# Inverse roots of two attentions: from powers on GpSimd to exponentials of half logarithms on ScalarE, products of ones in the early gaps, and new orders on four engines

## The reference

```python
x = x + layernorm(attention_A(layernorm(x)))
x = x + layernorm(stack_B(layernorm(x)))
```

```python
q = l2norm(q) * qs;  k = l2norm(k) * ksc        # t / max(norm(t), 1e-12)
q, k = rotary_xpos(q, k)
h = a * gelu(g, approximate=False)              # feed-forward part
```

## Time and profile before

| | us |
|---|---|
| median of 3 runs | 487.34 |
| lowest and highest | 486.87, 491.44 |
| the profiled execution | 492.14 |
| its span, first to last instruction | 490.3 |
| mean granted clock of TensorE, share of full speed | 0.979 |

### The profile page before, as it was taken

How to read it: one execution, slowest core, us unless ns; L and a number is a source line. 1 busy time by engine, 2 the same in 40 slices (tenths; PEclk the granted TensorE clock), 3 DMA queues, 4 the chain that set the end, 5 groups by cost and what they waited for, 6 DMA issues and landing times.

```text
span 490.3 us, 15662 instructions
## 1 busy us (share of the span) xinstructions
PE 452.1 (92%) x6258; PEld 288.7 (59%) x6258; DVE 380.0 (77%) x743; ACT 343.9 (70%) x901; POOL 320.7 (65%) x270
## 2 busy tenths in 40 slices
PE   7879989999989898999899999999998999998994
PEld 5656656656656565756455665565655655655662
DVE  3746675896898659989978788789688697877776
ACT  2136756575667898887768887887887788876832
POOL 4422150678559987999987986884978449773112
PEclk8879999999899999999999999999999999999998
DMA  6102022000001010010000000110000000101102
GB/s 192 45 3 47 14 86 47 5 10 17 3 4 24 3 24 1 4 23 1 23 3 23 23 3 21 23 23 3 23 1 23 1 23 1 23 2 24 23 1 86
DMA packets 13476, 11.42 MB, mean 23 GB/s; under 512 B 4210, under 2 KB 10716, under 8 KB 13404
## 3 DMA queue, kind: packets, MB, share of 16 engines
q1 hardware_dynamic: 13404, 10.42, 8.2%
HBM read 5.05 MB, written 1.05 MB: 12 GB/s over the span
## 4 chain that ended last, share of the span: by engine, by line
PE 57%; DVE 19%; ACT 9%; issue 8%; POOL 5%; DMA 2%; POOLq 0%; SPq 0%; DVEq 0%; ACTq 0%
PE bank L512 8%; PE bank L609 8%; PE bank L729 8%; ACT bank L1324 5%; PE bank L685 4%; PE bank L695 4%; DVE mx_a L1808 4%; PE bank L648 4%; PE bank L618 3%; PE bank L546 3%; PE bank L666 3%; PE bank L744 3%; DVE p_b L1890 2%; PE bank L629 2%; DVE rc L1864 2%
## 5 line engine op out<-in xcount | busy, mean ns | idle before, releaser
L2440 POOL TENSOR_TENSOR r_qk<-ss,minus_half 128x16 f32<-128x16 f32 x32 | 93.7, 2929 | 2.7
L1324 ACT ACTIVATE bank<-bank,mn_b 128x128 f32<-128x128 f32 x256 | 88.9, 363 | 3.1 <-DVE mn_b L1878 3.0
L2433 POOL TENSOR_TENSOR rc<-rc,rs 128x1024 f32<-128x1024 f32 x32 | 75.5, 2359 | 23.3 <-DVE rs L1870 23.3
L1808 DVE TENSOR_REDUCE mx_a<-bank 128x2 f32<-128x512 f32 (+1 forms) x96 | 61.3, 685 | 31.6 <-PE bank L523 31.1
L1277 ACT ACTIVATE pT_k<-bank 128x512 f32<-128x512 f32 x96 | 52.9, 598 | 34.8 <-PE bank L523 34.7
L2447 POOL TENSOR_TENSOR rc<-rc,r_qk 128x1024 f32<-128x1024 f32 x32 | 60.8, 1903 | 2.3
L609 PE MATMUL bank<-wqkv,xS 128*128 128x512 f32 x128 | 61.8, 605 | 0.3 <-DVE mx_a L1808 0.3
L1324 ACT ACTIVATION_READ_ACCUMULATOR bank<-bank,mn_b 128x1 f32 x256 | 58.8, 230 | 0.0
L512 PE MATMUL bank<-qT_a 32*128 32x256 f32 (+1 forms) x768 | 52.8, 368 | 4.2 <-ACT qT_a L1261 1.6
L1864 DVE TENSOR_TENSOR rc<-bank,tab_c 128x1024 f32<-128x1024 f32 x32 | 39.0, 1219 | 14.4 <-ACT sq L1299 14.0
L729 PE MATMUL bank<-yfT,w 128*128 128x512 f32 (+3 forms) x108 | 48.1, 559 | 0.4 <-ACT pT_b L1333 0.2
(11 more groups left out here) (136 smaller groups left out, 870.4 us busy)
## 6 DMA issues: line engine op xcount, KB each, us to landing
v_b<-v_b SPq DMA_DIRECT2D x32, 128.0 KB, 2.5
wqkv<-in_L_ffn_wqkv_dram SPq DMA_DIRECT2D x2, 768.0 KB, 5.6
x_all<-in_L_attn_x_dram SPq DMA_DIRECT2D x1, 768.0 KB, 5.6
out_dram<-pT_k SPq DMA_DIRECT2D x3, 256.0 KB, 2.3
w<-in_L_ffn_w_dram SPq DMA_DIRECT2D x2, 341.0 KB
wo<-in_L_ffn_wo_dram SPq DMA_DIRECT2D x2, 256.0 KB, 5.6
const<-consts_dram SPq DMA_DIRECT2D x1, 352.0 KB, 6.3
x_all<-in_L_attn_x_dram SPq DMA_DIRECT2D x1, 256.0 KB, 3.0
```

The costliest lines, as they stand in the source:

```text
L1324: m = s.activation(x, x, ACT.Exp, bias=mn_b[:, qt, c, p:p + 1], scale=-1.0, accum_out=sum_b[:, qt, c, p:p + 1])
L1808: v.tensor_reduce(mx_a[:, qt, h0:h0 + nh], full(src).rearrange("p (h k) -> p h k", h=nh), AX.X, ALU.max).then_inc(S("a_mx"), 1)
L2433: g.tensor_tensor(rc[:, k % 2, :, :], rc[:, k % 2, :, :], rs[:, k % 2, :, :], ALU.add).then_inc(S("b_add"), 1)
L2440: g.tensor_tensor(r_qk[:, n, :], ss[:, n, :], minus_half[:, :], ALU.pow).then_inc(S("b_r"), 1)
```

## The change

1. **Second attention's inverse norms.** DVE's b_norms takes the maximum with TINY itself, behind its sum. b_pow moves from POOL's list to ACT's: a logarithm in place, then an exponential with the scale -0.5.
2. **The two layer norms between the blocks.** a_z and a_h0 on POOL lose their powers; ACT has a_z_rs and a_h0_rs, each a logarithm and an exponential on 128x2.
3. **One table.** exps() loads the table that has both logarithm and exponential. It stands ten times in ACT's list, wherever such an operation follows other tables.
4. **Products of ones.** busy takes waits. Six calls of it are new in TensorE's list, with 2, 4, 3, 5, 2 and 2 products of 128 columns, all among the first three batches of the first attention.
5. **Orders.** The lists of TensorE, ScalarE, VectorE and GpSimd are new, and so are the banks. SP's list is the same. The powers of f_rs, last_rs and a_rs stay on POOL.

```diff
-            def busy(dst, n, cols):
+            def busy(dst, n, cols, *free):
+                for f in free:
+                    after(t, *f)
                 for _ in range(n):
                     t.matmul(full(dst)[:, 0:cols], ones[:, 0:PARTS], ones[:, 0:cols], start=True, stop=True)
...
+            def exps():
+                s.preload_act_table_set("natural_log_exp_and_others")
+            def a_z_rs(b):
+                s.wait_ge(S("a_ve0"), b + 1)
+                s.activation(rs2[0][:, :], ve2[0][:, :], ACT.Ln).then_inc(S("a_ln0"), 1)
+                s.wait_ge(S("a_ln0"), b + 1)
+                s.activation(rs2[0][:, :], rs2[0][:, :], ACT.Exp, scale=-0.5).then_inc(S("a_rs0"), 1)
...
+            def b_pow(k):
+                n = k % 2
+                s.wait_ge(S("b_ss"), k + 1)
+                s.activation(ss[:, n, :], ss[:, n, :], ACT.Ln).then_inc(S("b_ln"), 1)
+                s.wait_ge(S("b_ln"), k + 1)
+                after(s, *unit("b_qkr", k - 2))
+                s.activation(r_qk[:, n, :], ss[:, n, :], ACT.Exp, scale=-0.5).then_inc(S("b_r"), 1)
...
                 v.tensor_reduce(ss[:, n, :], sq[:, n, :].rearrange("p (h d) -> p h d", d=HD), AX.X, ALU.add)\
-                    .then_inc(S("b_ss"), 1)
+                    .then_inc(S("b_sum"), 1)
+                v.wait_ge(S("b_sum"), k + 1)
+                v.tensor_scalar(ss[:, n, :], ss[:, n, :], TINY, None, ALU.max).then_inc(S("b_ss"), 1)
...
             def a_z(b):
-                g.wait_ge(S("a_ve0"), b + 1)
-                g.tensor_tensor(rs2[0][:, :], ve2[0][:, :], minus_half[:, 0:TILES], ALU.pow).then_inc(S("a_rs0"), 1)
                 g.wait_ge(S("a_rs0"), b + 1)
...
-            def b_pow(k):
-                n = k % 2
-                g.wait_ge(S("b_ss"), k + 1)
-                g.tensor_scalar(ss[:, n, :], ss[:, n, :], TINY, None, ALU.max).then_inc(S("b_n2"), 1)
-                g.wait_ge(S("b_n2"), k + 1)
-                g.tensor_tensor(r_qk[:, n, :], ss[:, n, :], minus_half[:, :], ALU.pow).then_inc(S("b_r"), 1)
```

The new list of TensorE around the second batch of the first attention, and pieces of ACT's and DVE's:

```diff
+            a_turn_k(1, 7, of("a_mx", 0, 6, 12))
+            busy(0, 2, 128, of("a_mx", 0, 8, 12))
+            a_proj(2, 0)
+            busy(6, 4, 128, of("a_xnT_out", 2))
+            a_turn_m(0, 6)
+            busy(6, 3, 128, of("a_mT_out", 0), of("a_kT_out", 1))
+            a_turn_q(1, 3)
+            busy(7, 5, 128, of("a_qT_out", 1), of("a_rope", 2), of("a_mx", 0, 9, 12))
+            a_quad(1, 0, (7, 0, 5, 2))
...
+            b_proj(0, 0, of("a_exp", 2, 11, 12), of("a_mx", 3, 11, 12))
...
+            a_quad(4, 0, (7, 5, 3, 2), of("a_ov", 2, 0, 2), of("a_rope", 5), of("a_kT_out", 4))
...
             a_qT(1, 3)
+            exps()
+            a_exp(0, 0, 5)
...
+            f_gate(1, 1, 3)
+            exps()
+            b_pow(15)
+            b_pow(16)
...
+            b_rot(25, 3)
+            b_norms(25)
...
+            b_rot(26, 1)
+            b_norms(26)
```

More of the change, by code:

```diff
@@ L793, in _ @@
[L793 to L801, removed]
@@ L845, in _ @@
[L845 to L854, removed]
@@ new lines, in _ @@
+            a_values(4, 0, 7, of("a_rope", 7))
+            a_quad(5, 5, (6, 5, 0, 1), of("a_mx", 5, 7, 12), of("a_exp", 4, 8, 12), of("a_o", 3))
+            a_turn_q(6, 1, of("a_mx", 5, 9, 12))
+            a_values(4, 1, 7)
+            a_turn_o(3, 0, of("a_exp", 4, 10, 12))
+            a_turn_m(5, 6, of("a_mx", 5, 10, 12))
+            b_turn_qk(0, 1, of("a_qT_out", 6))
+            b_proj(2, 2, of("a_mx", 5, 11, 12))
+            b_v(2, 6, of("a_mT_out", 5))
+            a_values(4, 2, 3, unit("b_trT_out", 0))
@@ new lines, in _ @@
+            a_values(5, 1, 0)
+            a_h0(2, 6, of("a_exp", 5, 11, 12))
+            a_values(5, 2, 5, of("a_mx", 6, 9, 12))
+            a_turn_m(6, 1, of("a_mx", 6, 11, 12))
+            a_values(5, 3, 5)
+            b_v(3, 1, of("a_mT_out", 6))
+            a_turn_o(4, 4)
+            b_turn_p(0, 3, of("a_h0T_out", 2))
+            a_quad(7, 0, (4, 0, 5, 3), of("a_oT_out", 4), of("a_ov", 5, 1, 2), unit("b_p", 0))
+            b_turn_qk(2, 3, unit("b_pT_out", 0))
+            a_out(4, 1, unit("b_v", 3))
@@ new lines, in _ @@
+            b_turn_qk(5, 1, unit("b_o", 1), of("a_exp", 7, 4, 12))
+            a_turn_back(6, 0, of("a_exp", 7, 6, 12))
+            b_out(0, 7, of("a_yin", 5))
+            a_h0(4, 1, of("a_o", 6))
+            b_proj(6, 1, unit("b_trT_out", 5))
+            b_scores(3, 3, of("a_exp", 7, 7, 12), batch("b_x", 0))
+            b_turn_p(2, 0, of("a_h0T_out", 4))
+            b_proj(7, 0, unit("b_pT_out", 2))
+            b_values(2, 2)
+            b_v(5, 2, unit("b_rot", 6))
+            a_quad(8, 2, (3, 4, 7, 5), unit("b_o", 2), unit("b_p", 3))
@@ L1464, in _ @@
[L1464 to L1477 removed]
+            a_exp(1, 8, 1)
+            a_exp(1, 9, 2)
+            a_exp(1, 10, 4)
+            a_z_rs(0)
+            a_ov(1, 0, 3)
@@ new lines, in _ @@
+            a_exp(4, 5, 7)
+            a_h0T(1, 1)
+            a_kT(6, 5)
+            a_exp(4, 6, 3)
+            a_exp(4, 7, 2)
+            a_z_rs(2)
+            a_exp(4, 8, 5)
+            a_exp(4, 9, 4)
+            b_pow(1)
+            a_exp(4, 10, 0)
+            a_qT(6, 1)
+            a_exp(4, 11, 1)
+            a_ov(4, 0, 7)
+            a_oT(3, 0)
+            a_mT_out(5, 6)
+            b_qkT(0, 1)
+            b_sq(2, 2)
+            b_v(2, 6)
+            a_ov(4, 1, 3)
+            a_exp(5, 0, 6)
```

2201 lines of the change are left out of this document (1096 added, 1105 removed).

## The result

The changed kernel takes 500.8 us in the median of four runs (495.79 to 503.95), the kernel before beside it 488.1 us: a ratio of 1.0222 with a 95% interval of 1.0156 to 1.0288. The forecast was 481.7 us with a range up to 497: the time moved the other way, and it lies above the range. The first line is the engines' busy time, the second the chain of waits by engine.

A forecast was written before the change was run, and what follows sets the result against it. TensorE was taken as the bound, busy 452.1 of 490.3 us. Clock -2.1, 100 to 128 us -3.5, middle about 0 and tail 0 summed to -5.6 from the median of 487.34: 481.7 us, range 470 to 497.

The forecast's parts named there:

- item 3: Middle, 140 to 470 us: GpSimd's relief -5.7, VectorE's load +4.2, ScalarE's +3.0; net about 0, bounds -8 and +11.
- VectorE +22 x 0.19 = +4.2: Middle, 140 to 470 us: 22 us of maxima added on VectorE, weighted by its 19% share of the chain.
- rival C: VectorE's maximum waits for GpSimd's 128x1024 operations; half of 22 us reaches TensorE, 11 us more: 492.8 us; chance 0.20.
- item 1: Clock, 29 to 36 us: 2.7 us back from full-level quads, less the products' cost; net -2.1, bounds +1.3 and -3.3.
- Rival C's mark for VectorE's load: At 1.4 us per maximum for all units, VectorE has 314 us of work from 140 to 470, as much as TensorE.
- The seven units with the sum directly behind the rotation: Second attention's units 6, 9, 10, 20, 25, 26, 29: maximum waits for GpSimd's addition, 1.4 us each, 9.8 us.
- the six with one instruction between: Second attention's units 7, 8, 11, 13, 18, 19: maximum on VectorE at about 0.4 us each, 2.4 us.
- the other nineteen: Remaining units of the second attention: maximum put at L1834's mean, 0.53 us each, 10.1 us.
- Item 2: Stretch 100 to 128 us: TensorE's idle time and low clock, where two GpSimd powers stand; -3.5 us, bounds 0 and -4.
- The term for ScalarE (+3.0): Middle, 140 to 470 us: 33 us added on ScalarE by activation pairs and table loads, weighted by 0.09.
- Item 4: Tail: last gates, products, statistics and powers of last_rs stay; 0, within 2 us either way.
- Rival D: ScalarE at 90% in strict order makes late items delay all behind; 9.6 us more arrive: 491.3 us; chance 0.08.

The follow-up runs named there:

- No maximum at all: Changed kernel without VectorE's maximum with TINY, the reduction itself releasing ScalarE's logarithm: 484.0 us, ratio 0.9897 to the kernel before.

## Why the prediction was wrong, point by point

**The step that failed** is in item 3 of the sum: "VectorE +22 x 0.19 = +4.2". The mechanism was foreseen, the maximum waiting for GpSimd's 128x1024 operations, and so were its 22 us on VectorE (21.4); what was wrong is the weight. 15.5 of 21.4 us arrived, 0.72 each. With +15.5 in place of +4.2 the sum is +5.7, rival C's outcome; measured is +11.2 against the runs of before beside it (499.6 - 488.4). Of the rest, 2.1 us are item 1, of which nothing was there; more than that is not placed. Two things were wrong in the weight.

First, 0.19 is VectorE's share in the chain over the whole kernel. An average share says how often the end passed through that engine, not what a microsecond added in one place will cost. From 200 to 240 us VectorE had 3.2 us left, and with the maxima there 0.85. Rival C's mark for VectorE's load, 314 us of work in 330, was read over the long stretch and so was never reached on paper. The weight depends on the place: by the estimate under "No maximum at all" all of the waits between units 2 and 12 arrive, and about half of those behind unit 12; in the old order with the power on GpSimd it is 0.42 of the whole instruction.

Second, two of the waits end in the clock. The stalls at 184 and 238 us, behind a late p_b, were followed by windows down to 0.50; the rows above give 4.6 to 5.2 us for them, and without the maximum the clock is 1.00 in every window of 4 us from 140 to 300 us. Rival C priced the wait alone.

The 22 us themselves owe something to luck. The seven units with the sum directly behind the rotation were put at 9.8 us and had 6.9, since units 9 and 29 did not wait; the six with one instruction between were put at 2.4 and had 4.3; the other nineteen, at 10.1, had 10.2.

**Item 1, clock at 29 to 36 us, -2.1.** The level was kept as foretold (1.00 where the earlier trace rows had 0.64 and 0.51), and "2.7 us back" is about right for it: 2.96 us by the two timelines. The price of the products is what was mis-sized. They were taken to lie in TensorE's idle time but for half of 1.25 us. In fact they hold up the quad by 2.3 us, because TensorE's own turns stand behind them (a_turn_q starts at 25.44 us and not at 24.22), and the two at 47 us cost 0.6 more. Net it is 0 at 48 us.

**Item 2, 100 to 128 us, -3.5.** Right in kind: 120 to 124 us now has 3.96 us of TensorE at 1.00, where the earlier trace rows had 2.46, and no power is in the chain. The second attention's first scores start at 130 us and no longer at 149, which is the new order: with the powers back on GpSimd they start at 131 too. But the low level came at another place, 0.61 at 68 to 72 us, where the kernel before had 1.00, so that the mean from 40 to 140 us is 0.98 in both. The price of this item was not tested alone. The nearest is the kernel with the roots on ScalarE in the old orders and no maximum: its clock stays at 1.00 from 100 to 140 us, and from unit 0's sums to unit 3's it takes 41.1 us where the kernel before takes 42.9, 1.8 us less.

**Item 3, the rest.** Without VectorE's term the sum is -9.8, and without item 1 too -7.7. Measured is 0.9897 with no maximum, about -5 us, and 0.9809 with no maximum and no products of ones, about -9.3. The intervals are some 3 us to either side, so items 2 and 3 without the maximum hold together within what can be seen. The term for ScalarE (+3.0) is not separated from GpSimd's (-5.7), and its 33 us were 22 by the page. That GpSimd's share fell from 5% to 1% says nothing of its size in the new order, where the roots' place is worth 31 us: that order was made without the powers on GpSimd.

**Item 4, tail.** Nothing found against it.

**Rival D** did not come about in the new order, where ScalarE has 6% of the chain; in the old one with the roots put in by hand it has 19%, and the kernel loses 14.5 us without the maximum. The Trainium skill, page "ScalarE: Activation LUTs", section "What ACT_TABLE_LOAD costs", has a drain of about 1380 ns per switch beside the load; no trace here shows it: the idle time ahead of twenty loads is 0.4 us together.

**Rival C** was the right one, with a chance of 0.20. The Trainium skill, page "SBUF — State Buffer", section "Who interferes with whom", would have given the remedy too: it says that tensor_reduce never contends on trn2 and tensor_scalar can. The reduction of one element (0.170 us, never waiting) agrees. I cited the page for the wait and did not ask where in the kernel the waits would fall.

## What to carry to other kernels

Price an operation that is added to an engine by what stands behind it in the very stretch where it lands, not by the engine's average share in the chain: here the same waits weighed about half in one stretch and in full, with a fall of the clock on top, in another. Before a small elementwise operation goes from GpSimd to VectorE, look at what GpSimd runs beside it, and see whether the operation can be folded away: here a bias in the logarithm did it for 0.1 us. Busy work that is to keep TensorE's clock is only free if none of TensorE's own calls gets later by it; compare the start of a later, common instruction before paying for it.

## What the runs showed of the hardware

- A TENSOR_SCALAR of VectorE from SBUF to SBUF waits for all that is left of GpSimd's 128x1024 addition (2.36 us) or product (1.90 us); up to 2.30 us here. A TENSOR_REDUCE on the same operands doesn't wait (0.170 us, 32 of 32, in 16 of them with such an operation running all the way). Nor does a TENSOR_SCALAR that reads a PSUM bank (L1932 in the kernel before: 0.81 us twice inside a product, as at other times), nor one beside GpSimd's power of 2.93 us (0.17 us), nor the maximum at 127.48 us beside GpSimd's TENSOR_SCALAR of 128x128 (0.17 us).
- A bias from a tile makes an activation of 128x16 0.097 us longer (0.313 against 0.216). The pair of logarithm and exponential is 0.43 us where GpSimd's power takes 2.93.
- Two stretches in which TensorE idled for 2.48 us of 4 and for 2.85 us on end were followed by windows at 0.50 to 0.85 of the clock; with the waits gone 140 to 300 us reads 1.00 throughout. A shorter one, 1.64 us of 4 at 88 to 92 us, was followed by 0.65 to 0.79 in four kernels and by 1.00 in three.
